# Two attention blocks on one core: VectorE adds the eighth tile of exponentials onto GpSimd's sum of seven

## What is computed

```python
xn = group_norm(x)                                   # 32 groups
qkv = einsum('bchw,oc->bohw', xn, w_qkv) + b_qkv     # 8 heads of q, k, v, 32 channels each
m = softmax(einsum('bhcs,bhct->bhst', q * scale, k * scale), axis=-1)
a = einsum('bhst,bhct->bhcs', m, v)
out = x + einsum('bchw,oc->bohw', a, w_proj) + b_proj
```

## Time and profile before

| | |
|---|---|
| median of 3 runs | 2266.51 us |
| profiled execution, its own time | 2263.78 us |
| span of the profiled execution | 2262.0 us |
| mean granted TensorE clock (share of 2.4 GHz) | 0.986 |
| TensorE matmul busy | 97% of the span |
| VectorE, GpSimd, ScalarE busy | 75%, 79%, 56% |
| length of a slot | about 67 us, 32 of them |

### The profile page before, as it was taken

How to read it: one execution, slowest core, us unless ns; L and a number is a source line. 1 busy time by engine, 2 the same in 40 slices (tenths; PEclk the granted TensorE clock), 3 DMA queues, 4 the chain that set the end, 5 groups by cost and what they waited for, 6 DMA issues and landing times.

```text
span 2262.0 us, 41861 instructions
## 1 busy us (share of the span) xinstructions
PE 2193.9 (97%) x10552; PEld 1091.3 (48%) x10552; DVE 1692.7 (75%) x2896; ACT 1274.0 (56%) x2321; POOL 1788.2 (79%) x567
## 2 busy tenths in 40 slices
PE   5799999999999999999999999999999999999998
PEld 3355454545545455454544545445454544545442
DVE  3677787777877778777777878768777777877772
ACT  2355656566565555656555565655656556565554
POOL 2388878888887978878887888878878788788785
PEclk8799999999999999999999999999999999999999
DMA  4222233322333322233322333222333322433210
GB/s 118 57 69 49 53 95 76 95 43 56 72 75 96 68 68 53 57 95 94 89 40 63 81 76 94 62 61 55 71 94 76 79 45 51 93 76 76 52 43 20
DMA packets 208771, 157.53 MB, mean 70 GB/s; under 512 B 166528, under 2 KB 166784, under 8 KB 208512
## 3 DMA queue, kind: packets, MB, share of 16 engines
q1 hardware_dynamic: 208512, 154.48, 29.8%
HBM read 36.39 MB, written 16.78 MB: 24 GB/s over the span
## 4 chain that ended last, share of the span: by engine, by line
PE 89%; DVE 4%; issue 3%; SPq 1%; ACT 1%; DMA 1%; DVEq 1%; POOL 0%; ACTq 0%; POOLq 0%
PE ps_t L365 25%; PE ps_v L400 21%; PE ps_m L382 19%; PE ps_d L421 9%; PE ps_a L413 5%; PE ps_d L436 5%; PE ps_d L429 5%; SPq L254 1%; DVE raw_max L656 1%; DVE stage_ql L673 1%; DVE att L717 1%; ACT pt L582 1%; DVE rden L707 0%; DMA qs<-neg_max 0%; PE ps_m L421 0%
## 5 line engine op out<-in xcount | busy, mean ns | idle before, releaser
L656 DVE TENSOR_REDUCE raw_max<-ps_m 128x1 f32<-128x512 f32 x2048 | 1332.4, 684 | 444.1 <-PE ps_m L382 413.4
L582 ACT ACTIVATE pt<-ps_t 128x512 f32<-128x512 f32 x2048 | 1141.8, 596 | 919.3 <-PE ps_t L365 913.0
L828 POOL TENSOR_TENSOR acc<-acc,pt 128x2048 f32<-128x2048 f32 x317 | 1448.8, 4570 | 89.5 <-ACT pt L582 61.5
L382 PE MATMUL ps_m<-ks,qs 96*128 96x512 f32 x2048 | 988.0, 483 | 9.0 <-DVE raw_max L656 8.0
L365 PE MATMUL ps_t<-qs,ks 97*128 97x512 f32 x2048 | 879.0, 430 | 30.3 <-issue 13.1
L365 PEld LDWEIGHTS ps_t<-qs,ks 97*128 97x128 f32 x2048 | 389.6, 191 | 656.4 <-ACT pt L582 366.9
L828 POOL TENSOR_TENSOR acc<-pt 128x2048 f32<-128x2048 f32 x64 | 291.8, 4560 | 327.0 <-ACT pt L582 327.0
L400 PE MATMUL ps_v<-pt,v 128*32 128x512 f32 x4096 | 546.5, 606 | 0.0
L382 PEld LDWEIGHTS ps_m<-ks,qs 96*128 96x128 f32 x2048 | 393.0, 192 | 152.2 <-issue 62.7
L421 PE MATMUL ps_d<-xn,wq 128*128 128x512 f32 x500 | 262.7, 608 | 8.2 <-ACT xn L614 5.7
L400 PEld LDWEIGHTS ps_v<-pt,v 128*32 128x32 f32 x4096 | 80.7, 108 | 185.1 <-ACT pt L582 115.1
(11 more groups left out here) (46 smaller groups left out, 531.9 us busy)
## 6 DMA issues: line engine op xcount, KB each, us to landing
ks<-stage_kh SPq DMA_DIRECT2D x256, 128.0 KB, 2.5
qs<-stage_qh SPq DMA_DIRECT2D x256, 128.0 KB, 2.5
ks<-stage_kl SPq DMA_DIRECT2D x128, 128.0 KB, 2.5
qs<-stage_ql SPq DMA_DIRECT2D x128, 128.0 KB, 2.5
qs<-neg_max SPq DMA_DIRECT2D x1024, 0.5 KB, 2.0
xn<-x_dram SPq DMA_DIRECT2D x16, 512.0 KB, 4.0
res<-x_dram SPq DMA_DIRECT2D x16, 512.0 KB, 4.2
between<-res SPq DMA_DIRECT2D x32, 256.0 KB, 2.1
```

Source lines behind the costliest of these rows:

```text
L382: pe.matmul(ps_m[max_bank(u)][:, :], qs[b][0:KROWS, h, c:c + P], ks[b][0:KROWS, h, kf * HALF:(kf + 1) * HALF], start=True, stop=True).then ...
L582: act.activation(pt[t % 4][:, h, :], ps_t[u % 2][:, :], ACT.Exp, scale=SCALE).then_inc(exp_done, 1)
L656: dve.tensor_reduce(raw_max[:, e % 2, t, kf:kf + 1], ps_m[max_bank(u)][:, :], AX.X, ALU.max)\
L828: pool.tensor_tensor(acc[hf][:, :, :], a[:, :, :], pt[t % 4][:, :, :], ALU.add).then_inc(pool_added, 1)
```

## The change

One VectorE instruction is added for 63 of the 64 halves: `add_tail`, at u = 6 and u = 38 behind that step's `max_unit`. It adds `pt[3]`, the eighth tile, onto `acc` of the half that has just ended (128 x 2048 float32, both inputs and the output in SBUF). It waits for all exponentials of that half and for GpSimd's sixth add. `sums` then multiplies only `acc` with ones, 8 instructions in place of 16, and waits for the new semaphore `tail_added` in place of `pool_added`. ScalarE's exponential of the next tile 3 waits for `tail_added` in place of `sum_ready`. The last half is as it was.

```diff
+TAIL_AT = 6
...
-            def sums(s, hf, stats_done=None, pooled=POOLED):
+            def sums(s, hf, stats_done=None, pooled=NT):
...
-                pe.wait_ge(pool_added, ADDS * half + pooled - 1)
+                if pooled == NT:
+                    pe.wait_ge(tail_added, half + 1)
+                else:
+                    pe.wait_ge(pool_added, ADDS * half + pooled - 1)
                 aux_free(half, stats_done)
                 tiles = [pt[t % 4] for t in range(pooled, NT)] + [acc[hf]]
...
-                        act.wait_ge(sum_ready, half)
+                        act.wait_ge(tail_added, half)
...
+            def add_tail(half, hf):
+                dve.wait_ge(exp_done, HG * NT * (half + 1))
+                dve.wait_ge(pool_added, ADDS * (half + 1))
+                dve.tensor_tensor(acc[hf][:, :, :], acc[hf][:, :, :], pt[POOLED % 4][:, :, :], ALU.add).then_inc(tail_added, 1)
...
                     if has_next or AHEAD + u < UNITS:
                         max_unit(s.n, u)
+                    if u == TAIL_AT and not first:
+                        add_tail(NH * s.n - 1, NH - 1)
+                    if u == TAIL_AT + UNITS // NH:
+                        add_tail(NH * s.n, 0)
```

More of the change, by code:

```diff
@@ L211, in attention_layers @@
         pool_added = sem("pool_added")
+        tail_added = sem("tail_added")
         sum_ready = sem("sum_ready")
```

## The result

The changed kernel takes 2500.51 us (median; 2496.29 to 2503.89) against 2266.2 us before: ratio 1.1033, 95% interval 1.1010 to 1.1056, so 234 us slower. The forecast was slower by 184 us, 2450, with 2480 as the upper end. The direction was right, and so was the mechanism at both places. The term for the clock was much too small, a collision in the last slot had been put at nothing, and the measured time lies outside the range.

The account below looks back on a forecast made before the run. TensorE, busy 97% of the span, was taken to bound the kernel. -54.2 + 46.8 (u = 38) + 150.3 (u = 6) + 39 (clock) + 1.6 (end) = +183.5 us, giving 2450 us; range 2272 to 2480.

Parts of the forecast that it names:

- The gain of 0.86 us a half: TensorE's sums: 8 fewer matmuls with ones save 0.86 us a half, 54.2 us in 63 halves.
- Length of the addition, 2.27 us: VectorE's added instruction takes 2.27 us (bounds 0.672 and 2.69) and moves its queue back by 2.19 us.
- u = 38, the projection 1.56 us late: qk_low queues behind the addition, so TensorE's projection at u = 41 is 1.56 us late: 46.8 us in 30 halves.
- u = 6, side by side or standing: VectorE's addition waits out GpSimd's first add, making TensorE's u = 10 5.01 us late, 150.3 us; undisturbed, 0.83 us late.
- The clock, 39 us: TensorE's clock drops after each stand at u = 10, costing 1.3 us (bounds 0 and 1.60): 39 us in 30 halves.
- Slot 31, put at nothing: At u = 6 of slot 31 no collision with GpSimd was counted, only 0.8 us for the bank.
- The range: 2272 to 2480 us for 8 in 10; the forecast's own range was 2405 to 2480.
- Side by side: Rival: VectorE's and GpSimd's additions don't disturb each other; +18.6 us, 2285 us, chance 0.25.
- GpSimd's slack: GpSimd, held at u = 38, starts its next add about 0.6 us late, against a slack of at least 2.6 us.

Follow-up runs that it names:

- a2: Changed kernel, but the addition's second input is a PSUM bank, its output goes to its own tile, and TensorE sums two tiles; 2342.45 us.
- a5: Changed kernel, but the addition, both inputs still in SBUF, writes to its own tile and TensorE sums two tiles; 2522.98 us.
- a4: Changed kernel, with TensorE's stand at u = 10 filled by 18 matmuls whose result is overwritten; 2417.86 us.
- a1: Changed kernel, with GpSimd's first add of a half waiting for tail_added; 2293.27 us.
- c2: Against the kernel before: addition only in halves that end with a slot, as four one-head pieces at u = 4 to 7, GpSimd held until the fourth; 2253.36 us.
- d1: a1 with the second half's addition one step later, at u = 39, behind qk_low; 2270.77 us.
- a3: Changed kernel with both additions one step earlier, at u = 5 and 37; 2306.32 us.

## Why the prediction was right and wrong

**The gain of 0.86 us a half: right.** `sums` at u = 42 is 8 matmuls from 1114.80, and the next matmul starts at 1115.79: 0.99 us, against 1.85.

**Length of the addition, 2.27 us: right,** 2.28 where nothing collides, and it moves the queue back by 2.20 (1110.03 to 1112.23; the working had 2.19).

**u = 38, the projection 1.56 us late: right.** 1113.03, where 0.24 us behind the matmul of 1111.23 would be 1111.47: 1.56. The balance a half is 0.82 and not 0.70 away from the turns.

**u = 6, side by side or standing: right, and the judgement the sum rested on.** I had u = 10 late by 5.01 us; it went at 1152.49, where 1147.63 would be its time: 4.86. The rows of before could not decide this, and I said so. a2 and a5 are the pair that decides it.

**The clock, 39 us: this step failed.** I took 1.3 us a stand, from one slow stretch of 3.4 us behind a stand of 2.0 us, and named 1.60 as an upper bound. It was none: the stands at u = 10 had slow stretches of 6.8 us and more. From u = 10 to u = 12 the changed kernel takes 1152.49 to 1157.97 = 5.48 us. The kernel before would take 2.98 us for the same work: its 1043.97 to 1047.81 in its timeline, 3.84, less the 0.86 that is gone. That is 2.50 us lost in the stand shown, and a4 gives 2.7 as the mean of 31, 83 us in place of 39: 44 of the 50 us by which the forecast was short. I reasoned myself that a part of the slow stretch could fall into the stand and lowered the figure for that; the stretch did begin in the stand, and still reached 5.3 us past it.

**Slot 31, put at nothing: this was wrong too.** The prediction gave its first half 0.8 us for the bank, on the view that GpSimd's first add comes ahead of the addition in slots 1 to 30 only. The 31st collision makes that half 7.5 us longer than before. In a4, where the clock stays up, it is still 5.2 us longer. The other terms are small: u = 38 costs 3.6 us more than forecast (30 x 0.12) and u = 6 costs 4.5 less (30 x 0.15). Together, 44 + 5.2 + 3.6 - 4.5 = 48 of the 50 us; the last 2 are less than the runs' spread.

**The range: wrong for the same reasons.** Its top was built from 1.60 a stand. With 3 us a stand, which is known only now, it would have reached some 2500. Its ends are also a few us off what their terms add up to (2450 - 39 = 2411 for the lower, some 2484 for the upper), which decides nothing.

**The rivals.** Side by side was worked out as 2285; a1, which makes it true, is 2293. GpSimd's slack was judged rightly for slots 0 to 30: held for 1.3 us behind u = 38 (its first adds there take 5.8 us in place of 4.56), it is late for nothing. In slot 31 the addition does wait for it, 1.47 us.

## What to carry to other kernels

Before work is moved between VectorE and GpSimd, count the SBUF inputs on both sides at that very moment: two on VectorE against a GpSimd add (here with two SBUF inputs as well; one with fewer was not tried) means that the second to issue stands for the first, so place it where the other is idle, or make the less pressed one wait. Look at the last slot by itself: there one engine can wait for the other and so run into it. A long instruction on an engine with 25% idle time is a matter of who is queued behind it and when that is wanted, and pieces of a quarter of the length fit where the whole doesn't. And a stand of TensorE has a second price through its clock, which one stand elsewhere in the kernel doesn't bound; filling the stand with idle matmuls shows how large it is.

## What was not expected of the hardware

The slow clock behind a stand came in lengths of 3.4, 6.8 and 10.2 us. Behind 2.0 to 2.3 us of idle time in the kernel before it was 3.4 us (at five of the six places where the loop turns back, none at the first). In the changed kernel's 31 stands of 4.6 to 5.7 us it was 6.8 us (27) or 10.2 (4), and it always began while TensorE still stood. But the length of the stand alone doesn't give it: a5's 30 stands of 4.6 to 4.7 us had 6.8 us in 18 places and 3.4 in 12, a stand of 2.5 us in c2 had 6.8, and five of d1's six turns, with 1.9 to 2.6 us, had none. Kernels with nearly the same work differed through this by tens of us: a5 had 229.9 us of slow clock where the changed kernel had 290.9, with 504 matmuls more. What decides the length was not tried.

GpSimd is the one that stands if it issues second: its first adds of a half take up to 6.1 us in a3 in place of 4.56. While either stands, its record in the profile is a long busy one (6.32 us for an addition of 2.28) and not idle time.
